# Two adaptive-layer-norm layers: another shape, order and staging for the second attention's first pass

## The reference, cut to what matters

```python
q = rope((x @ Wqa @ Wqb).reshape(b, s, H, D))          # H = 16, D = 8
k, v = ...; k = rope(k)                                # 4 key heads, each repeated 4 times
scores = einsum('bqhd,bkhd->bhqk', q, k) * D ** -0.5
scores = where(causal, -inf, scores)
out = einsum('bhqk,bkhd->bqhd', softmax(scores), v).reshape(b, s, E)
return out @ Wout + bout
```

## Time and profile before

| | |
|---|---|
| runs | 1278.17 us median of 3 (1269.31 to 1282.07) |
| profiled execution | 1282.22 us, span 1280.4 us |
| mean granted TensorE clock | 0.917 |
| first score product to first step | 470.7 to 504.5 us |
| the 160 steps | 504.5 to 978 us |

### The profile page before, as it was taken

One profiled execution on the slowest core, in us unless ns is written; L12 is line 12 of the kernel. 1 busy time (PEld: TensorE's weight loads), 2 busy tenths in 40 slices (PEclk: granted clock), 3 DMA queues, 4 the chain that ended last, 5 costly groups with the idle time before them and its releaser, 6 DMA issues.

```text
span 1280.4 us, 17685 instructions
## 1 busy us (share of the span) xinstructions
PE 1148.3 (90%) x6034; PEld 620.2 (48%) x6047; DVE 928.0 (72%) x1803; ACT 756.3 (59%) x1112; POOL 174.5 (14%) x142
## 2 busy tenths in 40 slices
PE   3888668599999788999999999999997799999998
PEld 2333344477777423333233322322223688888886
DVE  4699986356555746688896869898932788888885
ACT  1635435477888322456565756566776666666664
POOL 0000000488899300000000000000000000000000
PEclk9898777899999865899997979998999799999999
DMA  5000011999985300000000000000000211111001
GB/s 166 1 0 1 0 46 30 220 228 217 200 192 128 132 1 1 2 2 2 2 1 2 2 1 2 1 1 1 2 1 1 93 58 58 58 58 57 0 2 33
DMA packets 37467, 64.01 MB, mean 50 GB/s; under 512 B 14346, under 2 KB 27914, under 8 KB 32010
## 3 DMA queue, kind: packets, MB, share of 16 engines
q1 hardware_dynamic: 37394, 63.04, 19.9%
HBM read 59.68 MB, written 3.21 MB: 49 GB/s over the span
## 4 chain that ended last, share of the span: by engine, by line
PE 62%; DVE 25%; ACT 5%; issue 4%; DMA 2%; POOL 1%; SPq 1%; DVEq 0%; POOLq 0%; ACTq 0%
PE ps L1069 10%; PE ps L862 9%; PE ps L864 9%; PE ps L863 9%; PE ps L998 7%; DVE arena_b L1815 6%; PE ps L1047 4%; PE ps L959 4%; DVE arena_b L1566 3%; PE ps L1011 2%; DMA arena_a<-root_weights 2%; PE ps L1054 1%; DVE arena_b L1747 1%; ACT arena_b L1379 1%; POOL parts L690 1%
## 5 line engine op out<-in xcount | busy, mean ns | idle before, releaser
L1379 ACT ACTIVATE arena_b<-ps 128x1024 f32<-128x1024 f32 (+3 forms) x320 | 275.1, 895 | 156.3 <-PE ps L1047 134.3
L862 PE MATMUL ps<-parts 128*128 128x512 f32 x640 | 254.3, 397 | 21.8 <-POOL parts L690 19.4
L863 PE MATMUL ps<-parts 128*128 128x512 f32 x640 | 250.5, 391 | 0.0
L864 PE MATMUL ps<-parts 128*128 128x512 f32 x640 | 250.3, 391 | 0.0
L1815 DVE TENSOR_REDUCE arena_b<-ps 128x1 f32<-128x512 f32 x384 | 237.6, 683 | 15.4 <-PE ps L998 14.0
L998 PE MATMUL ps<-arena_a 48*128 48x128 bf16 (+3 forms) x832 | 188.4, 324 | 10.8 <-DVE arena_b L1815 3.2
L690 POOL TENSOR_TENSOR parts<-arena_b,parts 128x512 fp32r<-128x512 f32 x128 | 166.4, 1310 | 70.5 <-ACT parts L1316 66.2
L1069 PE MATMUL ps<-arena_b 128*32 128x512 f32 (+3 forms) x1280 | 160.4, 575 | 0.0
L1047 PE MATMUL ps<-arena_a 50*128 50x512 bf16 (+3 forms) x832 | 152.6, 320 | 4.9 <-issue 2.6
L998 PEld LDWEIGHTS ps<-arena_a 48*128 48x128 bf16 x832 | 60.6, 97 | 186.1 <-DVE arena_b L1815 115.4
L1747 DVE SCALAR_TENSOR_TENSOR arena_b<-ps,arena_a 128x512 f32<-128x512 f32 x128 | 86.8, 688 | 87.7 <-PE ps L864 64.5
(11 more groups left out here) (265 smaller groups left out, 1172.5 us busy)
## 6 DMA issues: line engine op xcount, KB each, us to landing
arena_a<-root_weights SPq DMA_DIRECT2D x62, 512.0 KB, 7.8
arena_b<-expert_weights SPq DMA_DIRECT2D x7, 1024.0 KB, 6.7
wslot<-in_L_ffn_up_w SPq DMA_DIRECT2D x8, 256.0 KB, 7.0
wslot<-in_L_ffn_down_w SPq DMA_DIRECT2D x8, 256.0 KB, 9.1
root_weights<-arena_b SPq DMA_DIRECT2D x4, 512.0 KB, 7.0
wslot<-in_L_ffn_w_gate SPq DMA_DIRECT2D x8, 256.0 KB, 3.0
wslot<-in_L_ffn_w_up SPq DMA_DIRECT2D x8, 256.0 KB, 3.7
wslot<-in_L_ffn_w_down SPq DMA_DIRECT2D x8, 256.0 KB, 4.2
```

The lines of the kernel that those rows point to most:

```text
L862: mm(bank, w(0), x(0), start=start, stop=False)
L863: mm(bank, w(0), x(1), start=False, stop=False)
L864: return mm(bank, w(1), x(0), start=False, stop=stop)
L1379: a(probs[:, s % 2, 2 * pair:2 * pair + 2, off:CW], ps[:, 2 + 2 * pair:4 + 2 * pair, off:CW], ACT.Exp, scale=scale).then_inc(p2_exp, 1)
```

## The change

The scores of the first pass are made on all 128 rows. The key stack becomes two tensors, one with zeros in the upper half and one with zeros in the lower half; the query stack is used whole, and the zeros leave one head. Two GpSimd memsets write the zeros, at the end of the first layer's experts, and the first score waits for them. A key stack's copy is split into two halves of 64 rows. The second pass stays on its 50 rows. The items come in a new order: one of each size for group 0 upwards, then the other groups of chunk 3, of 2, of 1 and of 0. Stacks are made in the item ahead of the one that needs them, so three are left ahead of the first slot. Only the scores of the first item, four of the second and the first maxima are ahead of the first step. The bias addition on GpSimd waits for the maxima of four items. Buffers of maxima are reset where an item is smaller than the one that used the buffer before it. The slots beside the steps are now 16, 16, 6, 6, then 6 or 7 in item (1,0), 5 to 7 in (2,0), 4 or 5 in the long ones and (2,1), 3 in (2,2) to (1,2), fewer after that.

```diff
-NITEM = NC * G1
+ITEMS = ((0, 0), (1, 0), (2, 0), (3, 0), (3, 1), (3, 2), (3, 3), (2, 1), (2, 2), (2, 3), (1, 1), (1, 2), (1, 3),
+         (0, 1), (0, 2), (0, 3))
+NITEM = len(ITEMS)
...
+    stacks, needed = [], []
+    for c, g in ITEMS:
+        for x in [(a, g, 0) for a in range(c + 1)] + [(c, g, 1), (c, g, 2)]:
+            if x not in stacks:
+                stacks.append(x)
+        needed.append(len(stacks))
...
+        ahead = stacks[needed[n]:needed[n + 1]] if n + 1 < NITEM else []
...
-    slots = [scores[:end[1]]]
-    done = end[1]
+    end = {n: scores.index(("maxima", n)) + 1 for n in range(NITEM)}
+    done = end[0]
+    slots = [scores[:done]]
...
-        for n in range(2, NITEM):
+        for n in range(1, NITEM):
             if first[n] - 3 >= k:
-                want = min(end[n] + HPG + 1, len(scores)) - done
+                want = end[n] - done
...
-        kst = take([G1, T], BF16)
+        kst = take([2, G1, T], BF16)
...
-            pool.wait_ge(ln_xn, 3 * NC)
+            pool.wait_ge(moe_down, N_IT0 * MU)
+            pool.wait_ge(moe_prod, N_IT0 * MU)
+            g.memset(kst[STRIP:P, 0].rearrange("p g t -> p (g t)").bitcast(F32), 0.0).then_inc(kzero, 1)
+            g.memset(kst[0:STRIP, 1].rearrange("p g t -> p (g t)").bitcast(F32), 0.0).then_inc(kzero, 1)
+
+            pool.wait_ge(nm_ready, G1)
             pool.wait_ge(wo1_ready, 1)
...
-                    pe.wait_ge(stack_ready, 3 * (n + 1))
-                    r = slice(STRIP * (i % 2), STRIP * (i % 2) + KROWS)
+                    pe.wait_ge(stack_ready, NEEDED[n])
+                    if m == 0:
+                        pe.wait_ge(kzero, 2)
...
-                        return mm(b[:, at_:at_ + kw], qst[r, g, tq // TPC, i // 2, ...], kst[r, g, k0:k0 + kw],
+                        return mm(b[:, at_:at_ + kw], qst[:, g, tq // TPC, i // 2, ...], kst[:, i % 2, g, k0:k0 + kw],
...
-                    return mm(ps[:, 2 + 2 * pair + i, lo:hi], kst[r, g, j * P:(j + 1) * P],
+                    return mm(ps[:, 2 + 2 * pair + i, lo:hi], kst[r, i, g, j * P:(j + 1) * P],
...
-                    a(kst[:, g, chunk(c)], ps[:, bank, :], ACT.Identity, bias=onerow[:, :]).then_inc(stack_ready, 1)
+                    for half in range(2):
+                        r = slice(half * STRIP, half * STRIP + STRIP)
+                        last = a(kst[r, half, g, chunk(c)], ps[r, bank, :], ACT.Identity, bias=onerow[r, :])
...
+                    if n >= 2 and c < ITEMS[n - 2][0] and (...) and i == 0:
+                        chain(v.memset(mx[:, n % 2, :, :, 4 + c:7], -BIG))
```

More of the change, by code:

```diff
@@ L47 @@
 STRIP = 64
-NITEM = NC * G1
+ITEMS = ((0, 0), (1, 0), (2, 0), (3, 0), (3, 1), (3, 2), (3, 3), (2, 1), (2, 2), (2, 3), (1, 1), (1, 2), (1, 3),
+         (0, 1), (0, 2), (0, 3))
+NITEM = len(ITEMS)
+LAST_OF = {c: n for n, (c, g) in enumerate(ITEMS)}
 E1, F1 = 8, 512
@@ L61, in attention_schedule @@
 def attention_schedule():
-    steps = [(n, j) for n in range(NITEM) for j in range(TPC * (n // G1 + 1))]
+    steps = [(n, j) for n, (c, _) in enumerate(ITEMS) for j in range(TPC * (c + 1))]
     first = {}
@@ L71, in attention_schedule @@
         first.setdefault(n, k)
+    stacks, needed = [], []
[4 more added lines that the diff above has]
+        needed.append(len(stacks))
     scores = []
-    for n in range(NITEM):
-        c = n // G1
+    for n, (c, _) in enumerate(ITEMS):
         blocks = [("scores", t, u) for t in range(TPC * c, TPC * c + TPC) for u in range(c)]
         blocks += [("diag", 0, 0), ("below3", 0, 0), ("below12", 0, 0)]
+        ahead = stacks[needed[n]:needed[n + 1]] if n + 1 < NITEM else []
         for k, (what, t, u) in enumerate(blocks):
             scores += [(what, n, t, u, i) for i in range(HPG)]
-            if c < NC - 1 and (len(blocks) - 1 - k) < HPG - 1:
-                scores.append(("stack", -1, c + 1, n % G1, k + HPG - 1 - len(blocks)))
             if k == 0 and n > 0:
                 scores.append(("maxima", n - 1))
+            scores += [("stack", -1) + x for x in ahead[k * len(ahead) // len(blocks):(k + 1) * len(ahead) // len(blocks)]]
     scores.append(("maxima", NITEM - 1))
-    end = {n: max(k for k, x in enumerate(scores) if x[1] == n and x[0] != "maxima") + 1 for n in range(NITEM)}
-    slots = [scores[:end[1]]]
-    done = end[1]
+    end = {n: scores.index(("maxima", n)) + 1 for n in range(NITEM)}
+    done = end[0]
+    slots = [scores[:done]]
     late = {}
-    for n in range(NITEM):
-        s = first[n] + TPC * (n // G1 + 1)
+    for n, (c, _) in enumerate(ITEMS):
+        s = first[n] + TPC * (c + 1)
         late.setdefault(s + 1, []).append(("out", n))
-        if n % G1 == G1 - 1:
-            late.setdefault(s + 2, []).append(("turned", n // G1))
-            late.setdefault(s + 3, []).append(("product", n // G1))
+        if n == LAST_OF[c]:
+            late.setdefault(s + 2, []).append(("turned", c))
+            late.setdefault(s + 3, []).append(("product", c))
     for k in range(len(steps)):
         rate = 0
-        for n in range(2, NITEM):
+        for n in range(1, NITEM):
             if first[n] - 3 >= k:
-                want = min(end[n] + HPG + 1, len(scores)) - done
+                want = end[n] - done
                 rate = max(rate, -(-want // (first[n] - 2 - k)))
@@ L105, in attention_schedule @@
     tail = [x for k in sorted(late) for x in late[k]]
-    return steps, slots, tail
+    return steps, slots, tail, stacks, needed
 def adaln_two_layers(nc, A, out):
@@ L422, in adaln_two_layers @@
         out_ready = sem("out_ready")
-        STEPS, SLOTS, LAST_SLOTS = attention_schedule()
+        STEPS, SLOTS, LAST_SLOTS, STACKS, NEEDED = attention_schedule()
         NFIRST = len(SLOTS[0])
-        PRE = 3 * G1
-        STACKS = [(c, g, kind) for c in range(NC) for g in range(G1) for kind in range(3)]
+        PRE = NEEDED[0]
         def slot_bank(m):
@@ L441, in slot_before @@
             return ORDER[same[-1]] if same else None
+        assert [x[2:] for x in ORDER if x[0] == "stack"] == STACKS[PRE:]
         NITEM0 = min(k for k, x in enumerate(SLOTS[0]) if x[1] == 1 or x[0] == "maxima")
@@ L1024, in slot @@
                     c = what[1]
-                    pe.wait_ge(slot_read, READ["out", c * G1 + G1 - 1])
+                    pe.wait_ge(slot_read, READ["out", LAST_OF[c]])
                     for k, t in enumerate(tiles(c)):
@@ L1341, in stack_copy @@
                 else:
-                    a(kst[:, g, chunk(c)], ps[:, bank, :], ACT.Identity, bias=onerow[:, :]).then_inc(stack_ready, 1)
+                    for half in range(2):
+                        r = slice(half * STRIP, half * STRIP + STRIP)
+                        last = a(kst[r, half, g, chunk(c)], ps[r, bank, :], ACT.Identity, bias=onerow[r, :])
+                        if half == 0:
+                            step(last)
+                    last.then_inc(stack_ready, 1)
             slot_at = [0]
@@ L1812, in slot @@
                     _, n, t, u, i = what
+                    c = ITEMS[n][0]
+                    if n >= 2 and c < ITEMS[n - 2][0] and (what[0] == "scores" and (t, u) == (TPC * c, 0)
+                                                           or what[0] == "diag" and c == 0) and i == 0:
+                        chain(v.memset(mx[:, n % 2, :, :, 4 + c:7], -BIG))
                     m8 = mx[:, n % 2, 2 * (i % 2) + i // 2]
```

17 lines of the change are left out of this document (9 added, 8 removed).

## The result

The changed kernel takes 1303.77 us (median of 4, 1301.97 to 1304.71). The kernel before took 1274.10 us beside it, and the ratio is 1.0235, with a 95% interval of 1.0189 to 1.028: slower by some 2.3%. (The 1278.17 us of the kernel before were the median of three executions; a fourth of 1270.03 makes it 1274.10.) The forecast was 1295 in a range of 1255 to 1315. The profiled execution took 1303.25 us, against 1298.8 forecast for it.

A forecast was written before the change was run, and what follows sets the result against it. VectorE's row maxima bounded the kernel before; TensorE would bound most steps after. The profiled 1282.2 us, less 16.4 at the start, plus 33.0 in the steps, gave 1298.8, or 1295 for the median; range 1255 to 1315.

The forecast's parts named there:

- The price of a change of shape: TensorE: a 512-column product costs 0.213 us before its own shape and 0.32 us before a different one.
- The full step: Attention step away from the diagonal: 2.79 us on TensorE with four slots against VectorE's 2.49, and 2.58 with three.
- Rival 1: Prefetched weight loads hide the changes of shape, VectorE stays the bound at four slots: 1255 us for the median; chance 0.22.
- rival 2: The drain at a change of shape costs half, 20 of the 40 us: 1275 us; chance 0.20.
- TensorE became the bound: In attention steps with three, four and nearly five slots TensorE replaces VectorE as bound, by 0.30 us a step at four.
- The items, one by one: The attention's 160 steps, summed by item in the new order: 506.5 us against 473.5, so +33.0.
- The clock: Attention steps: full clock assumed because TensorE streams almost without a gap; the earlier half-clock stretches, costing 16 us, left out.
- rival 3: The clock falls again in the attention steps, costing 20 to 25 us where TensorE is the bound: 1317 us; chance 0.16.
- The order: New order of items: the lone second pass of 35 us shrinks to the last two one-chunk items; gain held in 506.5.
- the forecast's own formula: TensorE's time in a full step with k slots: 1.94 + 0.213k us, with six changes of shape instead of two.
- The start: Ahead of the first step: -12.2 us fewer stacks, -8.7 fewer scores, +1 one stack more, +3.5 memsets beside the normalization: -16.4.
- The offset of 4 us: The earlier kernel's median, 1278.2 us, lay 4 us below its profiled execution, so 1298.8 became 1295.

The follow-up runs named there:

- Grouping: Changed kernel with TensorE's slots in two groups instead of three, and ScalarE working both exponentials before any stack's copy: 1289.45 us, 1.013 times the kernel before.
- the burst: Changed kernel plus 112 unread 512-column products behind the attention, of like and alternating shapes; a change of shape took 0.11 us at half clock.
- the pair of the last experiment: Changed kernel with slots in two groups and second pass on 128 rows in diagonal steps only: old order of items 1269.59 us, new order 1276.06 us.

## Why the prediction was right, and where its sizes were off

**The price of a change of shape held.** 0.32 us against 0.213, read off two places of the earlier trace rows, was the base. The full step was forecast at 2.79 us for four slots and 2.58 for three; it takes 2.82 and 2.6. Grouping took 0.21 away, the burst showed 0.11 with nothing else around, and 128 rows in both passes left no gap between them. Rival 1 (the changes are hidden, decided by a step under 2.55 us) is refuted, and so is rival 2 (half of them): with half the price a step would take some 2.6 us. Of the Trainium skill, TensorEngine Tiling (Array Packing), Key Properties, says that a change of the tiling mode drains the engine; the runs agree and give the figure, 0.11 us per change. They add that 48 and 50 rows in one strip are one mode.

**TensorE became the bound**, as forecast: VectorE waits 0.34 us in a four-slot step (0.30 forecast), and 58.6 us in all ahead of its long reductions.

**The items, one by one**, from the first values of each (forecast, measured in us): (0,0) 33, 18.6; (1,0) 31, 32.9; (2,0) 43, 44.0; (3,0) to (3,3) 195 in all, 196.8; (2,1) 37, 36.0; (2,2) and (2,3) 68, 67.2; the three of (1,1) to (1,3) 71, 72.4; the last three 12, 8.5 and 8, measured 12.1, 9.5 and 5.5. All but the first are within 3 us of the forecast. The measured items add up to 495, not 512, as they begin with the first values and not with the first sums: the first 17 us, 14 of them at half clock, lie ahead of the first mark. Item (0,0) with them took 35.7 us where 33 was forecast.

**The clock.** That it would hold was assumed and gave rival 3 (it falls again, 1317) its place; it held, at 1.00 from 500 to 985 us. The forecast's reason, that TensorE now streams almost without a gap, doesn't set the new products apart: in the earlier trace rows the clock was at half with TensorE busy for 16.00 of 16 us. What held it is not known, so this part of the forecast was a guess that came out. What it gave back can be estimated: from the 48-row kernel to the 128-row kernel, both in the old order, the time at half clock in the steps fell from 39 us to 9, worth 11 us at 0.38 and at most 15, and the steps still grew by 20.9. So the shapes cost some 32 to 36 us, where rival 1's working had 40. Counted from the two programs' orders of products, with 64-row strips, 128x128 and 128x32 as the three shapes, the steps have some 780 changes on 48 rows and some 1085 on 128; 305 more at 0.107 are 33 us. Neither sum is shown by a run, as none had the shapes without the clock; the price of a step is.

**The order** was the step that failed. The forecast says that its sum "holds the gain of the order: the lone second pass of 35 us shrinks". It does shrink: the last three items take 27 us, and the last lone one 5.5. But the same kernel in the old order is 7 us faster. Where TensorE is the bound, its total counts and not VectorE's load, and two things in the new order add to it.

The first is in the forecast's own formula, 1.94 + 0.213k us for a step. It counts six changes of shape in every step. A step without slots has four fewer, and the old order has 17 such steps where the new one has 5. By the same count from the programs the new order has 44 changes more in the steps, an estimated 4.7 us, and 23 more in the pair of the last experiment, 2.5 us. With 128 rows in both passes a slot between the sums changes no shape; there the count is the same, and the order is worth 0.

The second is the first step. The new order puts 24 slots ahead of the first values and the old one 12, at a place that ran at half clock for 4 to 14 us. This is the old order with 128 rows:

```profile
484.74 0.29 PE L1061 MATMUL ps<-arena_a 50*128 50x128 bf16 x2 [3.09 <-DMA arena_a<-arena_b]
...
496.20 1.07 PE L1083 MATMUL ps<-arena_b 128*32 128x512 f32 x8
```

From the first sums to the first values it takes 11.5 us, and 17.2 in the changed kernel (to 501.16). In the pair with 128 rows in both passes it is 10.3 and 14.0, in the pair of the last experiment 12.1 and 15.7. Behind the first values the new order takes 0.8 us more, 3.4 less and 0.2 less in these three pairs, although it has 12 slots fewer left. That these two things make up the 7 us is an estimate; no run has one order with the other's changes.

On 48 rows slots and sums are one shape, the count is the same in both orders, and yet the new one costs 5 to 8 us. There the time at half clock in the steps rises from 39 to 79 us, worth 15 at 0.38, and the steps grow by 10.7. This is the likely cause there and not a shown one.

**The start**, forecast at -16.4, came to -19.3. From the experts' end to the first reduction it went from 46.1 to 36.1 us, by 10.0 where 12.2 less 3.5 was forecast. Most of the difference is the memsets:

```profile
424.30 3.51 POOL L708 MEMSET arena_a<- 64x4096 f32 x1 [1.08 <-PE ps L878]
427.86 3.50 POOL L709 MEMSET arena_a<- 64x4096 f32 x1
```

```profile
429.45 0.38 DVE L1488 BATCH_NORM_AGGREGATE mv<-stats 128x2 f32<-128x6 f32 x4
429.87 1.53 DVE L1491 TENSOR_SCALAR mv<-mv 128x4 f32<-128x4 f32 x1
429.94 1.45 DVE L1496 RECIPROCAL rstd<-sd 128x4 f32<-128x4 f32 x1
431.45 0.86 DVE L1498 TENSOR_SCALAR xn<-xt,mv,rstd 128x128 f32<-128x128 f32 x3
```

They are GpSimd's rows and VectorE's beside them. The size, 3.5 us each, and the mechanism were right: the scaling of 0.17 us takes 1.53 and ends at 431.4, when the second memset ends. The reciprocal behind it on VectorE ends then too, so that it can't be told whether it was held itself. But the chain had only begun to need VectorE's SBUF operations at 429.9. It lost 1.3 us (experts' end to the normalization's first scaling of tokens, at 431.45: 7.2 us against 5.9), not 3.5. The fewer stacks gave some 11.3 us, then, and not 12.2. From the first reduction to the first step it went from 32.9 to 23.6 us, by 9.2 where 7.7 was forecast, although the maxima's DMA showed more than the 1.5 that I gave it:

```profile
483.99 0.29 PE L1062 MATMUL ps<-arena_a 50*128 50x128 bf16 x2 [2.85 <-DMA arena_a<-arena_b]
```

The bias addition behind the fourth item's maxima took 4.52 us beside the steps and cost nothing to be seen. At its old place the stretched VectorE operation of 3.52 us took 0.69, and VectorE then idled 4.5 us for the keys' products: as forecast, no gain.

**The offset of 4 us** that took the forecast from 1298.8 to 1295 was wrong. The kernel before runs from 1264 to 1282, with its granted clock (0.931 to 0.916), and its profiled execution was one of the long ones. The kernel after runs within 3 us, with its profiled execution 0.5 from the median. An offset that belongs to one kernel's spread isn't the next one's. With it gone, the remaining miss on the profiled execution is 4.5 us: -2.9 at the start, +5.7 in the steps, -1.3 ahead of the attention, and +2.9 behind it, where 32 us instead of 21 ran at half clock. The medians differ by 29.7 us where 17 were forecast: 4 from the offset, 4 from the fourth execution of the kernel before, and the rest from the sum. That the median fell into the range owes something to the range's width of 60 us.

## What to carry to other kernels

Count the changes of tile shape in TensorE's order as instructions of their own, at 0.11 us each, before you widen one kind of product: 128 rows for one of three kinds of product cost 20 us here, and 128 rows for two of them, so that neighbours have the same shape, cost 3 (1279.6 against 1276.8 in the old order). When the change makes another engine the bound, go through the other parts of the same change again: an order that spreads VectorE's load over more steps gained nothing here once TensorE was the limit, and gave TensorE more changes of shape. And work shortened ahead of a loop goes into the loop: the start gained 17 us in the kernel on 48 rows, and its median was that of the kernel before.

## What the runs showed of the hardware

The granted clock isn't a matter of TensorE's busy time alone. In the earlier trace rows it fell to 0.51 and 0.50 in stretches that had TensorE busy for 16.00 of 16 and 16.67 of 17 us; with first-pass products of 48 rows, 39 to 79 us of the steps were at half in three kernels, and in seven with zero-padded products of 128 rows 4 to 20. The zeros' rows compute nothing, and still go with a higher clock. Which property of the products decides it wasn't isolated. A microsecond at half clock cost 0.38 us and not 0.5 in the kernel before, where VectorE bounds many steps. And GpSimd's memset held VectorE's scaling of 128x4 elements to its end, while BATCH_NORM_STATS2 and BATCH_NORM_AGGREGATE ran beside it at their usual time (the row at 429.45 took 0.38 us for four, during the second memset, as the same row of the kernel before did without one).
